# One multiply moved behind five DMA issues on ScalarE, in the expert loop of an AdaLN block

## The chip, the cores and the metric

The kernel runs on one core of a Trainium2 chip. The metric is device time in microseconds (us) from one launch, the median of several runs. Engines are named as in the profile: PE is TensorE, DVE is VectorE, ACT is ScalarE, POOL is GpSimd, SP is SyncE. "ACTq" rows are DMA issues by ScalarE's instruction queue.

## The reference, cut to what matters

The reference is one transformer block on x of shape (2, 4096, 512): layer norm and modulation, a linear-attention part, then a mixture of experts with 8 experts, of which each token takes two. The change touches the expert part alone:

```python
gate_out = ragged_dot(sorted_xs, w_gate, group_sizes=tokens_per_expert)   # 512 -> 2 x 512
activation = gelu(gate_out[:, 0, :]) * gate_out[:, 1, :]
expert_outputs = ragged_dot(activation, linear, group_sizes=tokens_per_expert)
out = einsum('blkd,blk->bld', expert_outputs per token, combine_weights)
x = x + gb * out            # gb: one row of 512 for each of the two batches
```

## The kernel before, in words

The program has three phases. The first makes keys and queries and splits the expert weights into a high and a low float32r part. The second finishes attention, routes the tokens and scatters token rows to one list per expert. The third, from about 1020 us to the end, is the expert loop; it walks 135 items (`ITEMS`), each one tile of 128 token rows of one expert. This text counts them 0 to 134, so the n-th row of any operation below that runs once per item belongs to item n-1.

For an item i the work is:

1. DVE turns the token rows (`turn_x`, L1597), ACT makes their high part (`x_hi`, L1015), DVE the low part (`x_lo`, L1603).
2. PE does the gate product and then the up product (`gate`, `up`: 12 matmuls each on L1721, three passes by four chunks).
3. ACT applies gelu to gate (`gelu`, L1020), DVE multiplies it with up (`glu`, L1609) into `hact`.
4. The activations have to be transposed. ACT stores `hact` to DRAM (`store_act`, one DMA, L1026, `act_rows<-hact`), later loads it back block by block in another order (`act_back`, four DMAs, L1033, `arow<-act_rows`), DVE transposes inside blocks (`turn_act`, L1615), ACT makes the high part (`act_hi`, L1039) and DVE the low part (`act_lo`, L1620).
5. PE does the down product (`down`, 12 matmuls, L1721 with `act_t_hi`).
6. DVE multiplies with the token's weight and its row of `gb` into `orow` (L1648), and POOL adds the rows to the output with an indirect DMA (L765). The row of `gb` is chosen by the token's batch: ACT makes `gb0`, the first batch's row times a 0/1 flag (`gb_rows`, L1045), and DVE adds the second batch's part (`gbr`, L1645).

The work is skewed over items by `LAG` = 3. In the loop's item i PE runs gate(i), up(i) and down(i-3). ACT runs `act_hi`(i-3), `gelu`(i), `x_hi`(i+1), `gb_rows`(i-3), `act_back`(i-1), `store_act`(i). DVE runs the small copies that end in `in_b` (`cur_of`, L1631 to L1635), `act_lo`(i-3), `turn_x`(i+1), `glu`(i), `x_lo`(i+1), `turn_act`(i-2), then `gbr` and `orow` of item i-3. Nothing but the order written in these functions sets the order on an engine; between engines there are semaphores.

The waits that matter here: `x_hi`(i+1) and `glu`(i) wait for up(i). `act_back`(i-1) waits until the store of item i-1 has landed in DRAM. `store_act`(i) waits for `glu`(i). `gb_rows` waits only for the flags of its item and for the `orow` of the item before. `gbr` waits for `gb_rows`, `orow` for down(i-3), and `act_lo` for `act_hi`. The down product waits for `act_lo`, the next gate product for `x_lo`. The weights of the next expert (three shares of about 3 MB and less) are loaded by SP's queue while items of the present one run.

Of the kernel before, what the change touches and what calls it, by code (L numbers as in the profile page):

```python
# [79 lines left out]
def at_least(eng, sem, value):  # L80

    if isinstance(value, int) and value <= 0:
        return
    eng.wait_ge(sem, value)
# [28 lines left out]
def build(nc, x, c_t, wmod, wqkv, wproj, b_proj, r_w, r_scale, pes, moe_w, out):  # L113
# [204 lines left out]
    def wait_apart(eng, sem, value):  # L318


        at_least(eng, sem, value)
        if not isinstance(value, int):
            eng.sem_inc(s_passed, 1)
# [450 lines left out]
    def _(act):  # L774
# [237 lines left out]
        def x_hi(i, at):  # L1012
            act.wait_ge(s_xt, i + 1)
            at_least(act, s_u, i)
            act.activation(x_t[0][:, :], XT_B[at % 2][:, :], ACT.Copy).then_inc(s_xthi, 1)  # L1015

        def gelu(i):
            act.wait_ge(s_g, i + 1)
            at_least(act, s_h, i)
            act.activation(gact[:, :], G_B[:, :], ACT.Gelu_apprx_tanh).then_inc(s_ga, 1)  # L1020

        def store_act(i, at):
            wait_apart(act, s_ar, 16 * NBLK * (i - RING + 1))
            wait_apart(act, s_h, i + 1)
            at = at % RING
            act.dma_start(ad[at * P:(at + 1) * P, :], hact[at % 2][:, :]).then_inc(s_hst, 16)  # L1026

        def act_back(i, at):
            wait_apart(act, s_ht, i - 1)
            wait_apart(act, s_hst, 16 * (i + 1))  # L1030
            at = at % RING
            for b in range(NBLK):
                act.dma_start(arow[at % 2][b * BLK:(b + 1) * BLK, :].rearrange("i (a n) -> i a n", a=NBLK),  # L1033
                              ad[at * P:(at + 1) * P, b * P:(b + 1) * P].rearrange("(a i) n -> i a n", a=NBLK)).then_inc(s_ar, 16)

        def act_hi(i):
            act.wait_ge(s_ht, i + 1)
            at_least(act, s_o, i)
            act.activation(act_t[0][:, :], HT_B[:, :], ACT.Copy).then_inc(s_hthi, 1)  # L1039

        def gb_rows(i, at):

            act.wait_ge(s_cur, 2 * (i + 1))
            at_least(act, s_or, i)
            act.activation(gb0[:, :], modbc[:, 0, 3, :], ACT.Copy, scale=in_b0[at % RING][:, 0:1]).then_inc(s_gb0, 1)  # L1045
# [6 lines left out]
        def item(i, at):  # L1052
            more = not isinstance(i, int) or i < ITEMS - 1
            lagging = not isinstance(i, int) or i >= LAG
            if lagging:
                act_hi(i - LAG)
            gelu(i)
            if more:
                x_hi(i + 1, at + 1)
            if lagging:  # L1060
                gb_rows(i - LAG, at - LAG)
            act_back(i - 1, at - 1)
            store_act(i, at)

        run_items(act, item)
        for i in range(ITEMS - LAG, ITEMS):
            act_hi(i)
# [985 lines left out]
```

## Time and profile before

| what | value |
|---|---|
| median of 3 runs | 2204.23 us (2200.72 to 2205.28) |
| the profiled execution's own time | 2204.23 us |
| span in its trace, first to last instruction | 2202.0 us |
| PE busy | 2082.6 us, 95% of the span |
| DVE, ACT, POOL busy | 60%, 36%, 36% |
| DMA queue q1 (SP), q10 (ACT), q0 (POOL) | 259.73, 70.82, 72.12 MB |

The profile is one execution. The span lies 2.2 us below the device time of the same execution. Busy time of PE is modelled and matmuls overlap. DMA issues are not counted as busy time of ACT; they stand in the timeline as ACTq rows, whose start is where the issue went out, not where data moved. In the timeline an entry may merge several instructions ("x3"); its second number is the time that it covers. A bracket at a row's end tells how long the engine was idle before it and what ended the idle time.

### The profile page before, as it was taken

How to read it: one execution, taken by the hardware profiler on the slowest of the kernel's cores; microseconds unless marked ns; L12 is line 12 of the kernel's file. 1: busy time of each engine (PE TensorE's matmuls, PEld its weight loads, DVE VectorE, ACT ScalarE, POOL GpSimd, SP SyncE). 2: the span in 40 equal slices, each digit the busy share in tenths (PEclk: the TensorE clock that was granted, in tenths of full speed). 3: DMA queues.
4: the chain of work that ended last, by engine and by line, in shares of the span. 5: the costliest groups of instructions: out<-in, count | busy, mean ns of one | idle time of the engine just before them, and what ended most of it. 6: DMA issues, size and time to landing. Idle time of an engine off the chain costs nothing.

```text
span 2202.0 us, 42565 instructions
## 1 busy us (share of the span) xinstructions
PE 2082.6 (95%) x9408; PEld 1618.8 (74%) x9409; DVE 1319.2 (60%) x3182; ACT 794.9 (36%) x1493; POOL 801.5 (36%) x618
## 2 busy tenths in 40 slices
PE   7999999999988999983999999999999989999997
PEld 4588887888855666662788888888878778888885
DVE  6555555556358787874555656565565555656554
ACT  3244443444335666651222222222222222222222
POOL 4466655665514667653111111111111111111111
PEclk9999999999989999996999999999999999999999
DMA  7575564556444767676855558558775975865554
GB/s 243 192 244 185 203 204 154 184 203 205 164 153 168 273 218 271 238 265 217 239 129 125 132 123 244 126 127 237 193 181 124 281 175 123 229 140 126 128 109 81
DMA packets 293689, 404.89 MB, mean 184 GB/s; under 512 B 50510, under 2 KB 188750, under 8 KB 285774
## 3 DMA queue, kind: packets, MB, share of 16 engines
q1 hardware_dynamic: 166256, 259.73, 37.0%
q0 software_dynamic: 30000, 72.12, 16.2%
q10 hardware_dynamic: 97200, 70.82, 10.1%
q14 instruction: 196, 1.61, 0.2%
q8 instruction: 37, 0.61, 0.1%
HBM read 210.57 MB, written 191.98 MB: 183 GB/s over the span
## 4 chain that ended last, share of the span: by engine, by line
PE 47%; DMA 3%; issue 1%; SPq 1%; ACTq 1%; DVE 0%; ACT 0%; POOL 0%; DVEq 0%; POOLq 0%
PE bank L1721 47%; DMA act_rows<-hact 2%; ACTq L1033 1%; DMA wbuf<-expert_split 0%; SPq L557 0%; DMA expert_rows<-rows,dest 0%; DMA out_rows<-orow,cur_tok 0%; DVE x_t_lo L1603 0%; DVE act_t_lo L1620 0%; ACT x_t_hi L1015 0%; DVE orow L1648 0%; SPq L555 0%; POOL expert_rows L744 0%; DMA arow<-act_rows 0%; DMA meta<-expert_rows 0%
## 5 line engine op out<-in xcount | busy, mean ns | idle before, releaser
L1721 PE MATMUL bank<-wbuf,x_t_hi 128*128 x2160 | 682.7, 397 | 33.5 <-DVE x_t_lo L1603 30.6
L765 POOL DMA_INDIRECT out_rows<-orow,cur_tok x135 | 209.0, 1548 | 971.8 <-DVE orow L1648 766.3
L1721 PEld LDWEIGHTS bank<-wbuf,x_t_hi 128*128 128x128 f32 x2160 | 409.0, 190 | 132.3 <-issue 35.4
L1721 PE MATMUL bank<-wbuf,x_t_lo 128*128 x1080 | 428.5, 397 | 0.0
L1721 PE MATMUL bank<-wbuf,act_t_hi 128*128 x1080 | 341.6, 397 | 13.4 <-DVE act_t_lo L1620 13.4
L1609 DVE TENSOR_TENSOR hact<-bank,gact 128x512 f32<-128x512 f32 x135 | 93.3, 691 | 379.6 <-PE bank L1721 369.9
L1721 PEld LDWEIGHTS bank<-wbuf,act_t_hi 128*128 128x128 f32 x1080 | 204.0, 189 | 64.8 <-issue 16.8
L1721 PEld LDWEIGHTS bank<-wbuf,x_t_lo 128*128 128x128 f32 x1080 | 204.7, 190 | 48.6
L1721 PE MATMUL bank<-wbuf,act_t_lo 128*128 x540 | 214.5, 397 | 0.0
L1015 ACT ACTIVATE x_t_hi<-bank 128x512 fp32r<-128x512 f32 x135 | 80.8, 599 | 299.2 <-PE bank L1721 285.3
L1039 ACT ACTIVATE act_t_hi<-bank 128x512 fp32r<-128x512 f32 x135 | 80.8, 598 | 289.7 <-DMA arow<-act_rows 202.6
L744 POOL DMA_INDIRECT expert_rows<-rows,dest x128 | 138.1, 1079 | 103.5 <-DVE dest L1424 69.1
L1020 ACT ACTIVATE gact<-bank 128x512 f32<-128x512 f32 x135 | 80.6, 597 | 252.6 <-PE bank L1721 232.3
L1122 DVE TENSOR_SCALAR hf<-bank,modcol 128x128 f32<-128x128 f32 x256 | 87.3, 402 | 94.5 <-PE bank L1701 94.4
L652 POOL TENSOR_TENSOR k_lo<-k_f,k_hi 128x512 fp32r<-128x512 f32 x64 | 89.0, 1390 | 122.3 <-ACT k_hi L817 122.2
L1721 PEld LDWEIGHTS bank<-wbuf,act_t_lo 128*128 128x128 f32 x540 | 102.3, 189 | 24.2
L648 POOL TENSOR_TENSOR z_lo<-xg,z_hi 128x512 fp32r<-128x512 f32 x64 | 83.3, 1304 | 98.2 <-ACT z_hi L806 98.2
L1648 DVE SCALAR_TENSOR_TENSOR orow<-bank,cur_w,gbr 128x512 f32<-128x512 f32 x135 | 101.4, 751 | 27.1 <-PE bank L1721 20.2
L1757 PE MATMUL bank<-k_hi,z_hi 128*128 128x512 f32 x256 | 104.4, 408 | 5.2 <-DVE kv L1206 2.9
L644 POOL TENSOR_TENSOR split_lo<-raw,split_hi 128x1536 fp32r<-128x1536 f32 x30 | 106.4, 3548 | 2.6 <-ACT split_hi L782 0.6
L1721 PE MATMUL bank<-kvp_hi,on_hi 128*128 128x512 f32 x256 | 103.5, 404 | 2.2 <-DVE on_lo L1525 2.2
L1597 DVE STREAM_TRANSPOSE bank<-xrow 128x512 f32<-128x512 f32 x135 | 96.8, 717 | 13.4 <-DMA meta<-expert_rows 13.4
(218 smaller groups left out, 3835.6 us busy)
## 6 DMA issues: line engine op xcount, KB each, us to landing
wbuf<-expert_split SPq DMA_DIRECT2D x24, 1536.0 KB
xrow<-expert_rows SPq DMA_DIRECT2D x540, 64.0 KB
act_rows<-hact ACTq DMA_DIRECT2D x135, 256.0 KB
arow<-act_rows ACTq DMA_DIRECT2D x540, 64.0 KB
expert_split<-split_hi SPq DMA_DIRECT2D x32, 768.0 KB, 3.6
expert_split<-split_lo SPq DMA_DIRECT2D x32, 768.0 KB, 5.9
xg<-in_x SPq DMA_DIRECT2D x16, 1024.0 KB, 5.4
q_rows<-qf SPq DMA_DIRECT2D x16, 1024.0 KB, 6.7
```

Of the source, the lines that this page charges most:

```text
L644: pool.tensor_tensor(sp_hl[1][:, :], raw[:, s, :], f32(sp_hl[0][:, :]), ALU.subtract).then_inc(s_elo, 1)
L648: pool.tensor_tensor(z_hl[1][:, t, :], xg[:, t, :], f32(z_hl[0][:, t, :]), ALU.subtract).then_inc(s_zlo, 1)
L652: pool.tensor_tensor(k_hl[t % 2][1][:, :], k_f[t % 2][:, :], f32(k_hl[t % 2][0][:, :]), ALU.subtract).then_inc(s_klo, 1)
L744: pool.indirect_dma_start(out=xs, out_offset=bass.IndirectOffsetOnAxis(dest[par][:, k, t:t + 1], 0), in_=rows[par][:, t, :], in_offset=Non ...
L765: pool.indirect_dma_start(out=out, out_offset=bass.IndirectOffsetOnAxis(cur_tok[at][:, 0:1], 0), in_=orow[at % 2][:, :], in_offset=None, c ...
L1015: act.activation(x_t[0][:, :], XT_B[at % 2][:, :], ACT.Copy).then_inc(s_xthi, 1)
L1122: last = ts(hf[t % 2][:, f, :], T_B[t % 2][:, f * P:(f + 1) * P], modcol[:, FC * B + at:FC * B + at + 1], modcol[:, at:at + 1], ALU.mult, ...
L1597: dve.transpose(XT_B[at % 2][:, :].rearrange("c (f a i) -> c a f i", f=FC, a=NBLK), xrow[at][:, :].rearrange("i (a f c) -> i a f c", a=NBL ...
L1609: tt(hact[at % 2][:, :], U_B[:, :], gact[:, :], ALU.mult).then_inc(s_h, 1)
L1648: stt(orow[at % 2][:, :], O_B[:, :], cur_w[at % RING][:, 0:1], gbr[:, :], ALU.mult, ALU.mult).then_inc(s_or, 1)
L1721: last = mm(dst, stationary(a, f), moving(b, f), start=(first and k == 0), stop=(k == parts * n - 1))
L1757: last = mm(ZK_B[f][:, :], z_hl[a][:, t, f * P:(f + 1) * P], k_hl[t % 2][b][:, :], start=(t == 0 and (a, b) == PASSES[0]), stop=(t == TPG ...
```

## The change

In the loop's item on ScalarE, `gb_rows`(i-3) is moved from ahead of `act_back`(i-1) and `store_act`(i) to behind them. The drain after the loop (`act_hi`, `act_back`, `gb_rows` for the last three items) is as before. All lines keep their numbers except these three in `item`.

```diff
             gelu(i)
             if more:
                 x_hi(i + 1, at + 1)
+            act_back(i - 1, at - 1)
+            store_act(i, at)
             if lagging:
                 gb_rows(i - LAG, at - LAG)
-            act_back(i - 1, at - 1)
-            store_act(i, at)
```

ScalarE, one item of the unrolled start of the expert loop (every later item reads alike). `act_stored` is the landing of the store, `act_ready` is `glu`, `down_done` the down product:

```order
 L1020 ACTIVATE gact<-bank2 128x512 [waits act_ready,gate_done]
 L1015 ACTIVATE x_t_hi<-bank5 128x512 [waits up_done,x_turned]
-L1045 ACTIVATE gb0<-modbc,in_b0_1 128x512 [waits out_rows_ready,cur_ready]
 L1033 DMA arow1<-act_rows 32x4x128 [waits act_stored,act_turned]
 L1033 DMA arow1<-act_rows 32x4x128 x3
 L1026 DMA act_rows<-hact0 128x512 [waits act_ready,act_rows_loaded]
+L1045 ACTIVATE gb0<-modbc,in_b0_1 128x512 [waits out_rows_ready,cur_ready]
 L1039 ACTIVATE act_t_hi<-bank1 128x512 [waits down_done,act_turned]
```

The multiply now stands behind a DMA that waits for a landing, and directly ahead of `act_hi`. The orders of PE, DVE, POOL and SP are unchanged.

VectorE, the engine that consumes `gb0`, before and now the same, in the last items of the loop. `gb0_ready` is the moved multiply, `gb_rows_step` the row after it:

```order
L1603 TENSOR_TENSOR x_t_lo<-bank0,x_t_hi 128x512 [waits up_done,x_hi_ready]
L1615 STREAM_TRANSPOSE bank1<-arow1 128x4x4x32 [waits act_lo_ready,act_rows_loaded]
L1645 SCALAR_TENSOR_TENSOR gbr<-modbc,in_b1_2,gb0 128x512 [waits cur_ready,gb0_ready,rows_added,out_rows_ready]
L1648 SCALAR_TENSOR_TENSOR orow0<-bank4,cur_w2,gbr 128x512 [waits gb_rows_step,down_done]
L1627 TENSOR_LOAD tables
L1627 ISA x2
L1631 ISA [waits rows5_loaded,rows_added,out_rows_ready]
L1631 COPY cur_w1<-meta5 128x1
L1632 COPY cur_tok5<-meta5 128x1
L1634 TENSOR_SCALAR in_b0_1<-cur_tok5 128x1 [waits cur_step]
L1635 TENSOR_SCALAR in_b1_1<-cur_tok5 128x1
L1620 TENSOR_TENSOR act_t_lo<-bank1,act_t_hi 128x512 [waits act_hi_ready]
```

Nothing moved here; the rows show what stands in line between `gbr` and the next `act_lo`, for which PE's down product waits.

## Rows read from the trace of the kernel before

**Rows 1.** The chain of waits over the whole span, its shares by line

```profile
by line: PE bank L1721 47.1%; DMA act_rows<-hact 2.4%; issue 1.0%; ACTq L1033 0.6%; DMA wbuf<-expert_split 0.4%; SPq L557 0.3%; DMA expert_rows<-rows,dest 0.3%; DMA out_rows<-orow,cur_tok 0.2%; DVE x_t_lo L1603 0.1%; DVE act_t_lo L1620 0.1%
```

**Rows 2.** Waits of PE, 1030 to 2202 us: total, times, longest

```profile
PE bank L1721 <- DVE act_t_lo L1620: 13.4, 7, 3.3
```

**Rows 3.** The chain of waits, 1500 to 1800 us: start, us, what

```profile
1600.65 9.06 DMA act_rows<-hact
...
1747.15 12.73 DMA act_rows<-hact
```

**Rows 4.** Timeline of a quiet item (46): start, us, engine, line, operation, idle before

```profile
1421.27 0.60 ACT L1015 ACTIVATE x_t_hi<-bank 128x512 fp32r<-128x512 f32 x1 [2.18 <-PE bank L1721]
1421.67 0.31 ACTq L1033 DMA_DIRECT2D arow<-act_rows  x1
1421.77 0.72 ACT L1045 ACTIVATE gb<-modbc,in_b 128x512 f32<-128x512 f32 x1
...
1423.69 0.34 ACTq L1026 DMA_DIRECT2D act_rows<-hact  x1
...
1421.30 0.69 DVE L1609 TENSOR_TENSOR hact<-bank,gact 128x512 f32<-128x512 f32 x1 [3.01 <-PE bank L1721]
...
1423.14 0.71 DVE L1645 SCALAR_TENSOR_TENSOR gbr<-modbc,in_b,gb 128x512 f32<-128x512 f32 x1
1423.99 0.75 DVE L1648 SCALAR_TENSOR_TENSOR orow<-bank,cur_w,gbr 128x512 f32<-128x512 f32 x1
...
1425.32 0.68 DVE L1620 TENSOR_TENSOR act_t_lo<-bank,act_t_hi 128x512 fp32r<-128x512 f32 x1
...
1429.66 0.69 DVE L1609 TENSOR_TENSOR hact<-bank,gact 128x512 f32<-128x512 f32 x1 [3.02 <-PE bank L1721]
...
1429.37 0.62 PE L1721 MATMUL bank<-wbuf,act_t_hi 128*128 x2
```

**Rows 5.** Timeline of ACT in item 1, where no gb_rows stands between

```profile
1044.60 0.60 ACT L1015 ACTIVATE x_t_hi<-bank 128x512 fp32r<-128x512 f32 x1 [2.25 <-PE bank L1721]
1044.63 1.78 ACTq L1033 DMA_DIRECT2D arow<-act_rows  x4
```

**Rows 6.** The chain of waits behind a late store, item 87

```profile
1784.58 0.34 ACTq L1026
...
1785.04 0.61 ACT act_t_hi L1039
...
1785.66 0.70 DVE act_t_lo L1620
...
1786.82 3.29 PE bank L1721 x13
```

**Rows 7.** Timeline of the last item: DVE waits for gb_rows there

```profile
2189.00 0.72 ACT L1045 ACTIVATE gb<-modbc,in_b 128x512 f32<-128x512 f32 x1 [0.19 <-DVE orow L1648]
...
2189.86 0.75 DVE L1645 SCALAR_TENSOR_TENSOR gbr<-modbc,in_b,gb 128x512 f32<-128x512 f32 x1 [0.32 <-ACT gb L1045]
```

**Rows 8.** Timeline: stores of items 3, 38, 57, and each next glu

```profile
1065.80 0.44 ACTq L1026 DMA_DIRECT2D act_rows<-hact  x1
...
1069.85 0.69 DVE L1609 TENSOR_TENSOR hact<-bank,gact 128x512 f32<-128x512 f32 x1 [1.55 <-PE bank L1721]
...
1359.44 0.34 ACTq L1026 DMA_DIRECT2D act_rows<-hact  x1
...
1362.74 0.69 DVE L1609 TENSOR_TENSOR hact<-bank,gact 128x512 f32<-128x512 f32 x1 [0.83 <-DMA act_rows<-hact]
...
1518.64 0.34 ACTq L1026 DMA_DIRECT2D act_rows<-hact  x1
...
1521.68 0.69 DVE L1609 TENSOR_TENSOR hact<-bank,gact 128x512 f32<-128x512 f32 x1 [0.23 <-PE bank L1721]
```

**Rows 9.** DMA queues, 1502 to 1503 us, weights loading: packets, MB, share of engines

```profile
q1 hardware_dynamic: 31, 0.38, 90.3%
q10 hardware_dynamic: 25, 0.05, 13.1%
```

## The prediction, made before the changed kernel ran

> **What bounds the kernel now.** I read the chain of waits first. By line it is mostly PE's products, and the largest piece that is not PE is a DMA, the store of the activations, 2.4% of the span [rows 1]. So the expert loop is bound by PE, and the only other thing that now and then takes over is the store's landing. Second, the waits of PE in the expert loop: it waits for `act_lo` 7 times, 13.4 us in all, the longest 3.3 [rows 2]; all other items run at PE's pace. Third, the chain between 1500 and 1800 us, which shows where: stores whose way to the next `act_back` took 9.06 and 12.73 us [rows 3]. Fourth, the timeline of a quiet item, to see how much room the other engines have [rows 4]: `glu` starts at 1421.30, the next at 1429.66, so the period is 8.36 us. The down product that needs this item's `act_lo` begins at 1429.37, which is 8.07 after `glu` and 0.29 before the next one. I call this moment D and measure lateness of everything against it.
>
> **The change in a quiet item.** ScalarE has the same 135 multiplies of 0.72 us and the same DMAs; nothing is added. Two things shift.
>
> First, the DMA issues come earlier. With `gb_rows` between, the first `act_back` goes out 0.40 us after `x_hi` began (1421.27 to 1421.67) [rows 4]; where no `gb_rows` stood between, 0.03 us after [rows 5]. The gain is at most 0.37 us and at least nothing. The loop body has a register operation there which the early item lacks, so I take 0.30. Note that it is not 0.72: the issue at 1421.67 goes out before the multiply begins at 1421.77, so the multiply's run itself never delayed the DMAs, only its dispatch. The store, now at 1423.69, will go at about 1423.39.
>
> Second, `gb_rows` comes later. It now follows the store's issue as `act_hi` did, 0.46 us after it (1784.58 to 1785.04) [rows 6], so at 1423.85 in place of 1421.77. `gbr` can follow 0.86 us after the multiply's start, read at the one place where DVE really waited for it [rows 7]: 1424.71 in place of 1423.14. `orow` follows `gbr` by 0.85 (1423.14 to 1423.99), `act_lo` follows `orow` by 1.33, with the four small copies between them [rows 4]. So `act_lo` starts at 1424.71 + 0.85 + 1.33 = 1426.89, 1.57 later than now. PE can start 1.16 after `act_lo`'s start (1785.66 to 1786.82) [rows 6], so at 1428.05, and D is at 1429.37. 1.32 us are left. A quiet item therefore costs nothing: the delay hides under the up product. It also gains nothing, since PE was never waiting there. The rows added to the output go out 1.6 us later; only POOL's next scatter waits for them, and `orow` two items on, for its buffer.
>
> **The change in a late item.** Here the path has no cover. `act_back`(i-1) sits on ScalarE's queue until the store of item i-1 has landed, and now `gb_rows` sits behind it. Before, the multiply, `gbr` and `orow` were all done in the shadow of that wait, and after the store's issue only `act_hi` and `act_lo` remained: from the store's issue to PE 1786.82 - 1784.58 = 2.24 us [rows 6]. Now DVE has `gbr`, `orow` and the small copies still in front of `act_lo`: 0.46 + 0.86 + 0.85 + 1.33 + 1.16 = 4.66 us. That is 2.42 more, against at most one early start of 0.30 for a run of late items: net 2.12. The chain from store to landing to `act_back` to next store does not itself pass through `gb_rows`, so within a run of late items the loss is not repeated; it is paid once, at the last.
>
> So an item costs something as soon as its store is issued later than D - 4.66, in place of D - 2.24. Item by item, D being the next `glu` less 0.29:
>
> Item 3, the first with a `gb_rows`: its store goes at 1065.80, set by a store of item 2 that nothing moved, so no early start is subtracted. 1065.80 + 4.66 = 1070.46 against D = 1069.56: 0.90 us [rows 8].
> Item 38: 1359.44 - 0.30 + 4.66 = 1363.80 against 1362.45: 1.35 us [rows 8].
> Item 57: 1518.64 - 0.30 + 4.66 = 1523.00 against 1521.39: 1.61 us [rows 8].
> The run of late stores that holds the 9.06 us landing, and the run that begins with the 12.73 us one and ends at item 87, both make PE wait already [rows 3, 6]: 2.12 each, 4.24.
>
> Sum: 0.90 + 1.35 + 1.61 + 4.24 = 8.1 us. The drain is not touched, except that the last loop item's `orow` may come a tenth later. Made against the profiled execution, 2204.23 us, which is also the median of the runs, this gives 2212.3 us.
>
> Bounds of the terms: with the early start at 0 or 0.37 in place of 0.30, the four last runs of lateness cost 1.2 more or 0.3 less. With `gbr` following the multiply by 0.72, its bare duration, in place of 0.86, all five cost 0.7 less. Each landing differs from run to run: the three times before lie 4.6 us apart, and the late items are the only place in the loop where I see such room.
>
> **A rule that bears on it.** While weights load, the two queues' packets move nearly one for one: 31 packets of q1 with 0.38 MB and 25 of q10 with 0.05 MB in one microsecond [rows 9]. So a store that meets a weight load waits for one large packet before each small one of its own. The Trainium skill states the same as a rule, in "DMA: Bandwidth & Descriptors", section "Queues, rings and completion order": each DMA engine goes round the queues that have work and switches at packet boundaries. By that rule a store that is issued 0.30 us earlier gets at most about one packet's turn ahead and still shares the engines for the rest; the 8.1 us would stand. Without it, if the earlier store simply went ahead of the weights, the second rival below would be the result.
>
> **The rivals.**
>
> *The late items thin out, no change.* The stores of items 38 and 57 are late by chance of where a weight share meets them. If their landings come 1.4 and 1.7 us sooner, both terms vanish, and if the three landings of the last run are 0.7 shorter each its 2.12 goes as well: 8.1 - 1.35 - 1.61 - 2.12 = 3.0, so 2207.2 us. For it: lateness in most of the loop is zero, and few items decide. Against it: nothing in the change makes landings shorter by more than the 0.30.
>
> *Faster: the store overtakes.* One mechanism: stores 0.30 earlier, and the scatter of output rows 1.6 us later, leave `act_rows` free of other traffic, and the landings of 9.06 and 12.73 us [rows 3] fall to what fits under the period. It decides from the point where the landings of a run shrink together by more than the 2.12 that the run costs. If it were complete, PE's waits for `act_lo` would go but for those of the drain. I put three of the 7 there, for its three last down products, at the mean of all: 13.4 x 4/7 = 7.7 goes [rows 2], and 2204.2 - 7.7 = 2196.5 us. Against it stand the packets that alternate [rows 9].
>
> *Slower by more: the scatter moves into the way.* Rows added 1.6 us later compete with the loading of the activations just stored, which was free of them. If some six stores in the crowded stretches land 1 us later each, that adds up to 6 us: 2218 us. For it: in such a stretch every microsecond of landing goes straight to PE. Against it: in quiet items there is room for it.
>
> **How the numbers follow.** The forecast, 2209 to 2216 us, gets 0.45. Thinned-out late items 0.28, overtaking 0.12, the scatter in the way 0.15. What can be told from no change here is about 0.2%, 4.4 us either way. The first and the last of these cases are slower by more than that, 0.60; the second is no change, 0.28; overtaking is faster, 0.12. The range that leaves out 2 in 10 is 2202 to 2218 us. Predicted is the likeliest, 2212.3 us.
>
> **What would show it.** In a quiet item of the changed kernel: first `act_back` issue about 0.1 us after `x_hi` begins; `gb_rows` about 2.5 us after `glu`, after the store; `orow` no longer started by PE's down product but by `gbr`, 1.5 us later than now; PE without a gap. In a late item: the chain of waits runs store issue, `gb`, `gbr`, `orow`, `act_lo`, PE, about 4.7 us in place of 2.2, and PE's waits for `act_lo` rise from 7 to about 10, their sum by about 8 us. The prediction is wrong if `gb_rows` never appears on the chain, if the landings of the stores change by more than 1 us on average, or if `gbr` follows quickly enough that `act_lo` still waits for `act_hi` last.

## The result, and the profile after

| | before | after |
|---|---|---|
| median of 4 runs | 2202.47 us (2196.64 to 2205.28) | 2227.73 us (2217.87 to 2236.43) |
| the profiled execution, its span | 2204.23 us, 2202.0 us | 2228.31 us, 2226.2 us |
| ratio after / before | | 1.0104, interval 1.0073 to 1.0137 |

The changed kernel is slower, as forecast, but by 25 us and not by 8; the time lies outside the range of the prediction. A second timing of the same kernel gave 1.0068 [1.0042, 1.0094], which is 15 us, so what has to be explained is 15 to 25 us.

**A quiet item.** The timeline of item 46 after the change, ACT first, then DVE (columns as in [rows 4], which show the same item before):

```profile
1434.12 0.60 ACT L1015 ACTIVATE x_t_hi<-bank 128x512 fp32r<-128x512 f32 x1 [2.19 <-PE bank L1721]
1434.36 1.83 ACTq L1033 DMA_DIRECT2D arow<-act_rows  x4
1436.44 0.34 ACTq L1026 DMA_DIRECT2D act_rows<-hact  x1
1436.96 0.72 ACT L1045 ACTIVATE gb<-modbc,in_b 128x512 f32<-128x512 f32 x1 [2.24 <-DMA arow<-act_rows]
1437.59 0.58 ACT L1039 ACTIVATE act_t_hi<-bank 128x512 fp32r<-128x512 f32 x1
...
1434.14 0.69 DVE L1609 TENSOR_TENSOR hact<-bank,gact 128x512 f32<-128x512 f32 x1 [1.15 <-PE bank L1721]
...
1437.81 0.75 DVE L1645 SCALAR_TENSOR_TENSOR gbr<-modbc,in_b,gb 128x512 f32<-128x512 f32 x1 [1.74 <-ACT gb L1045]
1438.67 0.75 DVE L1648 SCALAR_TENSOR_TENSOR orow<-bank,cur_w,gbr 128x512 f32<-128x512 f32 x1
...
1440.01 0.68 DVE L1620 TENSOR_TENSOR act_t_lo<-bank,act_t_hi 128x512 fp32r<-128x512 f32 x1
...
1442.54 0.69 DVE L1609 TENSOR_TENSOR hact<-bank,gact 128x512 f32<-128x512 f32 x1 [1.22 <-PE bank L1721]
```

The next `glu` comes 8.40 us after this one, so PE has its old pace. The first `act_back` goes out 0.24 after `x_hi` (0.40 before), the store 2.30 after `glu` (2.39 before), so the early start is 0.16 at the first DMA and 0.09 at the store (0.04 at the store in the median of all items). `gb` starts 0.52 after the store, `gbr` 0.85 after `gb`, `act_lo` 5.87 after `glu` where it was 4.02. The bracket behind `gbr` is new: DVE now waits for the multiply. Over the loop the waits of DVE (total us, times, longest) have this at their top, where before it came only once, in the last item, with 0.3 us:

```profile
DVE gbr L1645 <- ACT gb L1045: 225.5, 120, 5.1
```

**A late item.** The chain of waits after the change, item 68, behind three landings in a row, of 9.05, 8.98 and the 8.31 us in the first line; its own store was issued at 1631.35:

```profile
1620.83 8.31 DMA act_rows<-hact
...
1630.64 1.21 DMA arow<-act_rows
...
1631.87 0.73 ACT gb L1045
...
1632.72 0.76 DVE gbr L1645
...
1633.58 0.76 DVE orow L1648
...
1635.09 0.61 DVE act_t_lo L1620
...
1636.14 2.08 PE bank L1721 x7
```

From the store's issue to PE it is 1636.14 - 1631.35 = 4.79 us, against 2.24 in [rows 6]. In item 36 it is again 4.79. Over all items in which PE waits for `act_lo` it is 4.45 to 5.8 us in the two traces of after, and 2.2 to 2.6 in the two of before; the two waits behind store 57, in item 58, have 5.35 and 5.31.

**Where the time is.** The first and last rows of `glu` from item 3 to item 134 (131 periods), after and then before:

```profile
1067.99 0.69 DVE L1609 TENSOR_TENSOR hact<-bank,gact 128x512 f32<-128x512 f32 x1 [3.17 <-PE bank L1721]
...
2196.96 0.69 DVE L1609 TENSOR_TENSOR hact<-bank,gact 128x512 f32<-128x512 f32 x1 [1.87 <-PE bank L1721]
```

```profile
1061.48 0.69 DVE L1609 TENSOR_TENSOR hact<-bank,gact 128x512 f32<-128x512 f32 x1 [4.77 <-PE bank L1721]
...
2173.50 0.69 DVE L1609 TENSOR_TENSOR hact<-bank,gact 128x512 f32<-128x512 f32 x1 [3.69 <-PE bank L1721]
```

Against 131 quiet periods of 8.365 us (1095.8) the loop takes 33.2 us more after the change and 16.2 before. The second traces of each give 29.7 and 13.5. So the loop costs 16.6 us more in the mean of two traces each. In the profiled pair another 6.5 us lie ahead of item 3; there the traces of before differ by 5.2 among themselves (item 3 at 1061.48 and 1066.71), and the second trace of after has it at 1059.76, ahead of both, so I count none of that to the change.

Where a period was longer than the quiet one by over 0.5 us, in us, from the starts of `glu`:

| items | before, two traces | after, two traces | more, mean | my term |
|---|---|---|---|---|
| 4 | 0, 0 | 2.1, 0 | 1.0 | 0.90 (store of 3) |
| 37, 38 | 0, 0 | 3.7, 3.7 | 3.7 | 1.35 (store of 38) |
| 58 | 0, 0 | 2.1, 2.1 | 2.1 | 1.61 (store of 57) |
| 67 to 70 | 0.6, 4.6 | 8.7, 5.9 | 4.7 | 2.12 |
| 84 | 4.6, 3.9 | 7.4, 7.1 | 3.0 | none |
| 86 to 88 | 8.7, 4.6 | 3.9, 8.2 | -0.6 | 2.12 (run ending at 87) |
| 104, 106 | 0, 0 | 3.1, 1.1 | 2.1 | none |
| sum | | | 16.0 | 8.1 |

In item 84 PE waits for the next expert's weights in both kernels; the matmul that waits there is the gate product's first, which does not read `act_lo`. PE's waits in the loop, 1080 to 2180 us, after and then before:

```profile
PE bank L1721 <- DVE act_t_lo L1620: 15.7, 8, 2.5
PE bank L1721 <- DMA wbuf<-expert_split: 5.2, 1, 5.2
```

```profile
PE bank L1721 <- DVE act_t_lo L1620: 9.7, 5, 3.3
PE bank L1721 <- DMA wbuf<-expert_split: 2.8, 1, 2.8
```

That is 6.0 us more for `act_lo`, 2.4 more for weights; in the second traces it is 9.9 more for `act_lo` (15.5 and 5.6) and 2.7 more for weights (4.8 and 2.1). A wait of 2.1 us in item 4 of this trace of after lies ahead of the window. It is put down to the weights, but `act_lo` had started 1.13 us before PE went on, as in every wait for `act_lo`. A large part of the rest is clock. Item 38 after the change lost its time without waiting for anything: two stretches of it, and the same part of the loop before (columns: length, then busy us and instructions of PE, PEld, DVE, ACT, POOL, then the granted clock of PE, DMA share, GB/s):

```profile
1358.00:1360.00 2.00, 2.00 (x6) 1.61 (x5) 0.79 (x2) 0.17 (x1) 0.00 (x0) 0.50 1.03 381
1360.00:1362.00 2.00, 2.00 (x8) 1.54 (x8) 1.21 (x2) 1.15 (x2) 0.00 (x0) 0.70 0.94 257
```

```profile
1357.00:1361.00 4.00, 4.00 (x19) 3.25 (x18) 2.14 (x7) 1.05 (x2) 0.21 (x1) 1.00 0.84 144
```

At a granted clock of 0.50 (1.2 GHz of 2.4) PE completes 6 matmuls in 2 us, where before it had 19 in 4. PE had stood still for `act_lo` until 1356.62, for 1.88 us, and the clock fell after that. Where such a fall takes in an item without a wait of its own, the item is 1.8 to 1.9 us longer (item 38 in both traces of after, item 70 in one trace of each kernel, item 87 in one of after). Item 106 is not one of them: PE waited 1.95 us there at full clock. From item 4 to item 134 PE has 17.1 us at the half clock in each trace of after, and 6.8 and 10.2 in the two of before, so 3 to 5 us more are lost to it. In the profiled pair 6.0 + 2.4 + 2.1 + 5 = 15.5 of 17.0; the rest is in no row that I found.

**What the prediction did not have: the weights.** SP loads token rows and weights, and one item's weight share stands behind token rows that wait for the small copies (`in_b`, L1635). Those copies stand behind `orow` on DVE. Waits of SP in the loop, after and before:

```profile
SPq L323 <- DVE in_b L1635: 143.6, 82, 3.4
```

```profile
SPq L323 <- DVE in_b L1635: 120.7, 67, 5.7
```

The weight load in item 34, then the store of item 35 and the `act_back` that waits for its landing, after and before (`glu` of item 34 at 1329.77 and 1320.91):

```profile
1334.69 1.03 SPq L530 DMA_DIRECT2D wbuf<-expert_split  x2
...
1340.58 0.34 ACTq L1026 DMA_DIRECT2D act_rows<-hact  x1
...
1349.76 0.31 ACTq L1033 DMA_DIRECT2D arow<-act_rows  x1
```

```profile
1324.17 1.03 SPq L530 DMA_DIRECT2D wbuf<-expert_split  x2
...
1331.83 0.34 ACTq L1026 DMA_DIRECT2D act_rows<-hact  x1
...
1339.28 1.79 ACTq L1033 DMA_DIRECT2D arow<-act_rows  x4
```

The load starts 4.92 us after `glu` where it was 3.26, and the store lands in 9.18 us where it took 7.45. (A landing is read here from the store's issue to the first `act_back` behind it. In a quiet item that is 6.2 to 6.4 us whatever the store does, since `act_back` isn't due sooner.) The same holds behind other items at which a load starts: landings went from 7.5 to 9.1 (item 65) and from under 7 to 8.5 (item 102). That the queues share the engines is in [rows 9], 31 packets of q1 to 25 of q10. With the rule of the Trainium skill ("DMA: Bandwidth & Descriptors", section "Queues, rings and completion order") that an engine goes round its queues packet by packet, the longer landing fits with more of the load lying beside the store; no trace here shows how much did. I had used that rule only for the store's own 0.30 us, not for a load that moves 1.66; how long a landing gets, the rule does not give.

### The profile page after: what moved, and what is told of

Read it like the earlier page. It is cut to its first block, busy times and chain, and to the rows that moved or that the text cites. A ratio compares the mean times of both kernels' runs of the same rounds, so it can differ in the third digit from the quotient of the medians.

```text
span 2226.2 us, 42565 instructions
## 1 busy us (share of the span) xinstructions
PE 2096.0 (94%) x9408; PEld 1630.7 (73%) x9409; DVE 1343.1 (60%) x3182; ACT 794.8 (36%) x1493; POOL 802.0 (36%) x618
## 3 DMA queue, kind: packets, MB, share of 16 engines
q14 instruction: 196, 1.61, 0.2%
## 4 chain that ended last, share of the span: by engine, by line
PE 43%; DMA 5%; SPq 2%; issue 1%; ACTq 1%; DVE 1%; POOL 0%; ACT 0%; DVEq 0%; POOLq 0%
PE bank L1721 43%; DMA act_rows<-hact 3%; DMA out_rows<-orow,cur_tok 1%; ACTq L1033 1%; SPq L557 1%; DMA wbuf<-expert_split 1%; DVE gbr L1645 0%; DVE orow L1648 0%; ACT gb L1045 0%; DVE act_t_lo L1620 0%; SPq L555 0%; POOL expert_rows L744 0%; DMA arow<-act_rows 0%; SPq L559 0%; DMA expert_rows<-rows,dest 0%
## 5 line engine op out<-in xcount | busy, mean ns | idle before, releaser
L1645 DVE SCALAR_TENSOR_TENSOR gbr<-modbc,in_b,gb 128x512 f32<-128x512 f32 x135 | 101.5, 752 | 254.3 <-ACT gb L1045 232.8
L1045 ACT ACTIVATE gb<-modbc,in_b 128x512 f32<-128x512 f32 x135 | 97.7, 724 | 338.3 <-DMA arow<-act_rows 170.7
```

Source lines behind the costliest of these rows:

```text
L1645: gbs.did(stt(gbr[:, :], modbc[:, 1, 3, :], in_b1[at % RING][:, 0:1], gb0[:, :], ALU.mult, ALU.add))
```

## The experiments

The table has each kernel's median, its ratio to the kernel before on the same chip with the interval, the start of item 34's weight load after `glu`, and the landing of item 35's store (where another item is named, of that item's store).

| kernel | us | ratio | weights start | landing |
|---|---|---|---|---|
| after_again | 2217.67 | 1.0068 [1.0042, 1.0094] | 4.85 | 8.87 |
| before_again | 2203.86 | 1.0001 [0.9982, 1.0020] | 3.25 | 7.86 |
| pre_late | 2205.03 | 1.0018 [0.9993, 1.0042] | 3.22 | 7.4 |
| pre_early | 2202.87 | 1.0000 [0.9982, 1.0018] | 3.25 | 7.2 |
| orow4 | 2216.54 | 1.0084 [1.0056, 1.0112] | 4.94 | 9.0 |
| lo_first | 2224.59 | 1.0114 [1.0091, 1.0137] | 6.3 | 10.4 |
| orow4_lo | 2221.12 | 1.0098 [1.0067, 1.0129] | 6.3 | 10.2 |
| back_first_pre | 2221.83 | 1.0115 [1.0084, 1.0145] | 3.0 | 8.8 |
| cur_late | 2213.85 | 1.0037 [1.0015, 1.0059] | 4.1 | 8.1 |
| cur_later | 2207.99 | 1.0005 [0.9986, 1.0025] | 4.4 | 8.4 |
| cur_early_a | 2234.25 | 1.0141 [1.0113, 1.0169] | 2.4 | 6.9; item 55, load at 0.5: 14.9 |
| cur_early_b | 2220.12 | 1.0068 [1.0043, 1.0093] | 1.2 | item 34: 12.9 |
| cur_early_pre | 2223.56 | 1.0097 [1.0069, 1.0125] | 1.2 | item 34: 13.0 |
| cur_mid | 2231.26 | 1.0121 [1.0092, 1.0150] | 4.4 | 8.3 |
| shares4_b | 2234.60 | 1.0130 [1.0104, 1.0156] | | |
| shares4_a | 2241.87 | 1.0169 [1.0140, 1.0197] | | |
| wfirst_b | 2211.22 | 1.0024 [0.9995, 1.0054] | 4.2 | 7.8 |
| wfirst_a | 2219.22 | 1.0066 [1.0037, 1.0094] | 4.4 | 8.6 |

### The two kernels again

No edit but an empty line at the end of the file.

> The changed kernel once more, for a second trace. In its first trace the expert loop began 6.5 us later than in the trace of before, for a reason that lies ahead of the changed lines, and the loop itself took 17 us more. If the late start is chance, this trace starts its loop at another time and the median stays at 2218 to 2236 us; if the change causes it (code placed elsewhere), the loop starts near 1067 us at item 3's glu again.

> The kernel before once more, for a second trace: 2197 to 2206 us. If the number of late stores is chance, their items and landings differ from those of the first trace, while the sum of PE's waits in the loop stays under 20 us.

The loss is real and its size is 15 to 25 us; the kernel before against itself shows nothing. The late start of the loop was chance.

### Keep the early DMAs, take the multiply out of DVE's way

`gb0` gets two buffers, and the multiply is made one item ahead. In pre_late it stands where the change put it, behind the store; in pre_early ahead of the DMAs, where it was.

```diff
+            act_back(i - 1, at - 1)
+            store_act(i, at)
+            if ahead:
+                gb_rows(i - LAG + 1, at - LAG + 1)
-            if lagging:
-                gb_rows(i - LAG, at - LAG)
-            act_back(i - 1, at - 1)
-            store_act(i, at)
```

> gb_rows stands behind the DMAs as in the changed kernel, but works one item ahead (item i-2) into one of two buffers, so VectorE finds its result ready. Theory A (what costs is that gbr, orow, the scatter and act_lo wait for gb_rows): back to 2198 to 2207 us. Rival B (the DMAs sent 0.1 to 0.3 us earlier collide with other traffic): stays above 2218 us. Rival C (the multiply now ahead of act_hi on ScalarE delays act_hi by about 0.6 us in late items): 2206 to 2212 us.

> gb_rows one item ahead into one of two buffers, but ahead of the DMAs as in the kernel before. Theory A: VectorE did not wait for it before, so no change, 2197 to 2206 us. It is the control for the two buffers: if it moves, the look-ahead itself does something.

PE's waits in the loop of pre_late:

```profile
PE bank L1723 <- DVE act_t_lo L1622: 7.4, 3, 3.1
PE bank L1723 <- DMA wbuf<-expert_split: 2.4, 1, 2.4
```

The loss is gone within the interval, which leaves room for 0.42%, with the DMAs issued as early as in the change and the multiply at the same place in ScalarE's queue; in the trace the loop takes 9.9 us over its quiet pace, against 16.2 and 13.5 before. DVE's 225 us of waiting for `gb` are gone too, and the weight load is back at 3.22. So the cause is `gbr` waiting for the multiply, with everything that this wait delays. The earlier DMAs do neither good nor harm that this measurement shows, and pre_early against pre_late says the same.

### Is it the buffer of orow?

The chain of waits of after passes several times through the scatter of output rows, as here in item 36:

```profile
1347.60 5.61 DMA out_rows<-orow,cur_tok
1353.21 0.75 DVE gbr L1645
```

That reads as if `gbr` waited for the scatter to free its buffer. orow4 gives the buffer four copies.

```diff
-            at_least(dve, s_add, 16 * (i - 1))
+            at_least(dve, s_add, 16 * (i - 3))
...
-            stt(orow[at % 2][:, :], O_B[:, :], cur_w[at % RING][:, 0:1], gbr[:, :], ALU.mult, ALU.mult).then_inc(s_or, 1)
+            stt(orow[at % 4][:, :], O_B[:, :], cur_w[at % RING][:, 0:1], gbr[:, :], ALU.mult, ALU.mult).then_inc(s_or, 1)
```

> The changed kernel with four buffers for orow in place of two. gbr and orow then wait for a scatter two items older, so the 20 us in which gbr waited for out_rows in both traces of the changed kernel should be gone, while gbr still waits for gb_rows. Theory A1 (both waits feed PE's stalls: the late gb_rows and, on top, the scatter's landing): part of the loss returns, 2207 to 2213 us, with PE's waits for act_lo reduced but longer than before. Rival A2 (the order gb_rows, gbr, orow, act_lo is all that matters): no change from the changed kernel, 2216 to 2220 us. Rival A3 (the scatter's landing is all): 2202 us.

Waits of DVE in orow4:

```profile
DVE gbr L1646 <- ACT gb L1046: 223.5, 120, 6.8
...
DVE gbr L1646 <- DMA out_rows<-orow,cur_tok: 24.6, 9, 3.9
```

It is as slow as the change, and the wait is still put down to the scatter, 24.6 us, although now a scatter two items further back would have to be late. It was a false releaser: in every one of these items `gb` started 0.83 to 0.86 us before `gbr`, which is the delay of the quiet items (0.85). `gbr` waits for the multiply always.

### Take act_lo's way out instead

lo_first makes `act_lo` ahead of `gbr` and `orow` on DVE, and gives the down product a second bank. orow4_lo is both edits.

```diff
-            if lagging:
-                act_lo(i - LAG)
...
                 turn_act(i - LAG + 1, (at - LAG + 1) % DEPTH)
+                act_lo(i - LAG + 1)
             if lagging:
                 out_rows(i - LAG, (at - LAG) % DEPTH)
```

> The changed kernel, but VectorE makes act_lo(i-2) before gbr and orow of item i-3, and the down product has two banks so that it needn't wait for orow. gb_rows is as late as in the changed kernel, gbr still waits for it and for the scatter. Theory A (the loss reaches PE through act_lo queued behind gbr and orow): back to 2198 to 2206 us, although gbr goes on waiting. Rival (the late scatter harms by its traffic, in landings of the stores): stays above 2210 us.

> Both at once: four orow buffers, and act_lo ahead of gbr. Theory A: as lo_first within 3 us, since a wait of gbr no longer reaches PE in either. If the scatter's wait also delayed glu and x_lo of the next item, this is 3 us or more faster than lo_first.

PE's waits in lo_first:

```profile
PE bank L1720 <- DVE x_t_lo L1603: 8.7, 7, 1.9
PE bank L1720 <- DMA wbuf<-expert_split: 7.8, 1, 7.8
PE bank L1720 <- DVE act_t_lo L1620: 4.2, 4, 1.5
```

The waits for `act_lo` are down from 15.7 to 4.2, and the kernel is as slow as the change. `orow` and the small copies now come later still, so the weight load starts at 6.3 and the store lands in 10.4; and DVE gets to the next tokens late (`x_lo`). The edit moved the loss and did not remove it, and my expectation for it was wrong. With four buffers on top (orow4_lo) it is the same within the intervals. It is no clean test of `act_lo`'s way, but it was the first sign that the small copies matter by themselves.

### The store ahead of the next tokens

```diff
             gelu(i)
+            act_back(i - 1, at - 1)
             if more:
                 x_hi(i + 1, at + 1)
-            act_back(i - 1, at - 1)
```

> gb_rows one item ahead into two buffers, behind the store, and act_back(i-1) moved ahead of x_hi(i+1), so that the store of item i no longer stands behind four DMA issues (1.9 us). A store is then issued about 1.6 us earlier after glu and late stores have that much more room. If the late stores' chain is what is left of PE's waits, 2192 to 2199 us; rival: act_back now holds up x_hi when a landing is late, so PE waits for x_lo in place of act_lo and nothing is gained, 2200 to 2206 us.

```profile
PE bank L1723 <- DVE x_t_lo L1605: 13.6, 7, 2.9
PE bank L1723 <- DMA wbuf<-expert_split: 1.8, 1, 1.8
```

Slower by 1.15%, where no loss had been expected. The DMA that waits for a landing now holds back `x_hi`, and PE waits for `x_lo` 7 times where it had waited for `act_lo`. It is the same lesson in another place: what stands behind the waiting DMA inherits every late landing.

### The small copies and the weight loads alone

cur_late moves the copies of the kernel before behind `act_lo` and `turn_x`, so that the weights start later with `act_lo` as early as ever. cur_later adds a spare multiply ahead of them.

```diff
-            cur_of(i - 1, (at - 1) % DEPTH)
             if lagging:
                 act_lo(i - LAG)
             if more:
                 turn_x(i + 1, (at + 1) % DEPTH)
+            ts(spare[0][:, :], modbc[:, 0, 3, :], 1.0, None, ALU.mult)   # cur_later alone
+            cur_of(i - 1, (at - 1) % DEPTH)
```

> The kernel before, with only the small copies of cur_of (L1631 to L1635) moved on VectorE behind act_lo and turn_x, about 1.3 us later. gb_rows, gbr, orow and act_lo are as early as before or earlier. Theory P (SP's queue waits for these copies before it loads the rows of a later item, and the weight loads stand behind that; a weight load that starts later meets the store of the activations): the weight load of item 34 starts 1.3 us later than in the kernel before (3.3 us after glu there), the store of item 35 lands about 1.3 us later, and the time rises by 3 to 10 us. Rival Q (the loss comes only from act_lo waiting behind gb_rows, gbr and orow): no change or faster, 2197 to 2203 us.

> As cur_late (the kernel before with the copies of cur_of behind act_lo and turn_x), with a spare 128x512 multiply ahead of the copies that writes to a buffer of its own: a second dose. gb_rows, gbr, orow and act_lo are as early as before. The weight load of item 34 starts about 4.9 us after glu, as in the changed kernel. Theory P: the loss is larger than cur_late's 0.37%, 8 to 16 us over before, with landings of 9 us in items 35, 56, 65, 102 as in the changed kernel. Rival: no more than cur_late.

PE's waits in cur_later:

```profile
PE bank L1723 <- DMA wbuf<-expert_split: 6.0, 1, 6.0
PE bank L1723 <- DVE act_t_lo L1621: 3.3, 1, 3.3
```

Landings grow (8.1 and 8.4, against 8.9 and 9.2 in the change), item 84 is longer (8.3 and 8.6 us against 3.9 to 4.6), and no period at items 37, 58 or 104 is long; the loop costs 13.5 and 13.8 us over its quiet pace, as before. By the timings late weights alone cost between nothing (cur_later) and 0.4% (cur_late), and the 8 to 16 us expected for cur_later didn't come. The one with the smaller delay came out slower, and neither load starts as late as the 4.9 us of the change, so I take no more from the pair than "a few us at most, for half to 0.7 of the delay".

The opposite: the copies of item i ahead of `gbr`, in after (a), before (b) and pre_late (pre).

```diff
-            cur_of(i - 1, (at - 1) % DEPTH)
...
                 turn_act(i - LAG + 1, (at - LAG + 1) % DEPTH)
+            cur_of(i, at)
             if lagging:
                 out_rows(i - LAG, (at - LAG) % DEPTH)
```

> The changed kernel, with the copies of cur_of(i) moved ahead of gbr, so that SP no longer waits for orow while act_lo still stands behind gb_rows, gbr and orow. Theory P and the lateness of act_lo together: the weight load of item 34 starts no later than 3.3 us after glu, the store of item 35 lands as early as in the kernel before, and the time falls from 2218 to 2203 to 2211 us; what is left is act_lo's part, worth up to 8 us. Rival Q: stays at 2215 us or more, less 0.4 us per late item for the shorter way from orow to act_lo.

> The kernel before, with the copies of cur_of(i) ahead of gbr. Theory P: SP's weight loads start about 1.7 us earlier than in the kernel before, PE's wait for the weights (3.9 to 4.6 us in four traces) becomes 1.7 us shorter and late stores are fewer: 2192 to 2200 us. Rival Q: no change, 2198 to 2204 us.

> gb_rows one item ahead into two buffers and behind the store (pre_late), and the copies of cur_of(i) ahead of gbr. Theory P: like cur_early_b, 2192 to 2200 us, since neither VectorE's wait nor SP's is left. If gb_rows ahead of act_hi on ScalarE costs something in late items, up to 3 us slower than cur_early_b.

PE's waits in cur_early_b:

```profile
PE bank L1721 <- DVE act_t_lo L1620: 13.5, 4, 4.2
PE bank L1721 <- DMA wbuf<-expert_split: 1.8, 1, 1.8
```

All three got slower than the kernel they came from, by 0.4 to 0.8% by the ratios, where each had been expected to be faster. In cur_early_b and cur_early_pre the weights start 1.2 us after `glu`, ahead of this item's own store, which then takes 12.9 us (issued 1336.28, `act_back` at 1349.16 in cur_early_b); PE stalls behind the stores of items 34, 55, 64 and 101, 3 to 4 us each in cur_early_b. In cur_early_a the load of item 34 came at 2.4 and the stores of items 34 and 35 landed within 6.4 and 6.9; behind the other three, where it came at 0.5, PE stalls 5.6 to 6.9 us each. The wait for the weights themselves is 1.8 us in cur_early_b and 4.7 in cur_early_a. So the landing goes with the start of a weight load relative to the store: 12 to 15 us at 0.5 to 1.2, 6.9 to 7.7 at 2.4, 7.5 at 3.3, 9 at 4.9, 10.4 at 6.3. The kernel before, with most of its loads at 2.4 to 3.3, sits in the good place. As a test of the change these kernels fail, since they add a stall of their own.

cur_mid tried to put the copies at the old distance by letting them wait for the multiply:

```diff
             if lagging:
+                dve.wait_ge(s_gb0, i - LAG + 1)
+            cur_of(i, at)
+            if lagging:
                 out_rows(i - LAG, (at - LAG) % DEPTH)
```

> The changed kernel, with cur_of(i) ahead of gbr but made to wait for gb_rows first, so that it ends about 4.1 us after glu, as in the kernel before. gb_rows, gbr, orow and act_lo are as late as in the changed kernel. If the start of the weight loads relative to the stores carries the loss, the weight load of item 34 starts 3.0 to 3.6 us after glu, the store of item 35 lands within 8 us, and the time is 2 to 8 us above before (2 to 8 being what act_lo's way alone costs by the prediction's sum). Rival Q (act_lo's way carries it all): 14 us or more above before.

Inconclusive: the extra wait pushed `act_lo` to 6.8 us after `glu` in the median item, which takes all but 0.1 us of its room (PE's down product starts at 8.07 and needs it 1.16 sooner), and the load moved only from 4.9 to 4.4.

### Smaller weight shares

```diff
-SHARES = (GATE_UP[0:2], GATE_UP[2:3], DOWNS)
+SHARES = (GATE_UP[0:1], GATE_UP[1:2], GATE_UP[2:3], DOWNS)
```

> The kernel before, with the next expert's weights asked for in four shares, one an item, in place of three (the first of 3 MB is cut in two of 1.5 MB). If 3 MB bursts against stores are what makes landings late, late stores become fewer: 2 to 8 us faster than before. Rival: the last share comes an item later and PE waits longer for the weights of the short expert: same or slower.

> The changed kernel with the same four shares. If a burst met at a bad moment is the cause, smaller bursts take away most of the difference between the two orders: within 8 us of shares4_b. Rival Q: the difference of 15 us remains.

PE's waits in shares4_b, then in shares4_a:

```profile
PE bank L1721 <- DMA wbuf<-expert_split: 39.7, 2, 26.3
```

```profile
PE bank L1721 <- DMA wbuf<-expert_split: 22.5, 2, 15.2
PE bank L1721 <- DVE act_t_lo L1620: 17.0, 5, 5.5
```

Four shares take one item more to load, and a short expert's successor is not there in time: 39.7 us of waiting. No wait for `act_lo` is left in b, 17.0 us in a. The expected gain didn't come. The change costs 0.39% on top of b here, though the two intervals overlap.

### The same weight timing for both

In both kernels SP issues the weights ahead of the token rows and waits for the same event, a moment that lies ahead of `orow`'s copies.

```diff
         def step(i, at):
-            load_rows(i, at)
+            wait_apart(sp, s_h, i - AHEAD + 1)
             next_weights(i - AHEAD)
+            load_rows(i, at)
```

> The kernel before, but SP's step waits for glu of the item in hand and asks for weights first, and only then loads the rows of the item seven ahead. The weight loads are then paced by glu and no longer by the copies of cur_of; the load of item 34 starts about 3 us after glu. Close to the kernel before, 2196 to 2210 us: it is the base for wfirst_a.

> The changed order on ScalarE with the same step on SP: weight loads start as in wfirst_b within 0.3 us, while act_lo still stands behind gb_rows, gbr and orow. The difference to wfirst_b is what act_lo's way costs by itself. If it is all of the loss: 14 us or more over wfirst_b. If the late weight loads are a part: 5 to 11 us over wfirst_b. If it costs nothing without them: within 4 us.

PE's waits in wfirst_b, then in wfirst_a:

```profile
PE bank L1722 <- DMA wbuf<-expert_split: 8.5, 1, 8.5
PE bank L1722 <- DVE act_t_lo L1621: 6.0, 2, 3.0
```

```profile
PE bank L1722 <- DVE act_t_lo L1621: 6.6, 6, 2.1
PE bank L1722 <- DMA wbuf<-expert_split: 5.4, 2, 4.1
```

With the weights at 4.2 and 4.4 us, the change costs 8.0 us by the medians and 0.42% (9 us) by the ratios; the two intervals overlap, so this is a size and not a proof. The traces don't confirm it as a sum: the loop takes 21.1 us over its quiet pace in wfirst_a and 18.9 in wfirst_b, only 2.2 of the 7.6 us by which the two spans differ. Nor are the loads at one timing everywhere: wfirst_b asks for one share only in item 83 (wfirst_a in 82), and its item 84 costs 10.3 us where that of wfirst_a costs 6.7. The places are plainer than the sum: wfirst_a has long periods at items 37 (1.3), 58 (1.5) and 104 (0.6), wfirst_b has none there. (The trace puts the 1.3 us of item 37 down to the weights; `act_lo` had started 1.13 us before PE went on, so it is a wait for `act_lo`.) One item shows why. Behind the landing of item 35, the store of item 36 is issued so long after its `glu`: 3.70 us in before (4.09 in its second trace), 4.08 in wfirst_b, 4.75 in cur_later, 4.78 in wfirst_a, 5.33 in after. With the short way it may go until 8.07 - 2.24 = 5.83, with the long way until 8.07 - 4.79 = 3.28. So cur_later loses nothing (4.75 under 5.83), wfirst_a at nearly the same moment should lose 1.5 (measured 1.3), after 2.0 (1.8), and after with its store as early as in before would lose 0.4 (0.8 by the second trace). At this item the long way makes the loss possible, and by this reckoning the later weights make most of its size.

The output rows go out later in wfirst_a than in wfirst_b, and its landings over 7 us are not longer in sum: together they exceed 7 by 15.6 us, in wfirst_b by 21.8. That of item 35 alone is longer, 8.6 for 7.8.

## Why the prediction was wrong in size

**Right: the mechanism and who pays.** The change costs PE time only where a landing is late, through `gb`, `gbr`, `orow`, the small copies and `act_lo`. Removing `gbr`'s wait alone removes the loss (pre_late). The way measured 4.79 us at its plainest against 4.66 forecast; quiet items cost nothing, as forecast; item 58 lost 2.1 us for 1.61. PE's waits for `act_lo` rose by 6.0 and 9.9 us in the two pairs of traces, for the 8 forecast.

**Luck.** Item 4 lost 2.1 us in one trace and nothing in the other, so its mean of 1.0 for 0.90 says little. The term of 2.12 for the run ending at item 87 was not met: items 86 to 88 lost 0.6 us less than before. Item 84, for which the sum has no term, lost 3.0 more in the wait for weights and the slow clock behind it, and the two nearly cancel. In the trace before, PE already waited 2.8 us for these weights, and the prediction, which names the waits for `act_lo` alone, does not mention it. The 8 to 9 us of the timings with weights asked for first lie near the 8.1, but their traces put only 2.2 of it into the loop, so they don't confirm the sum.

**Wrong, the step that failed: "Item by item".** I took the set of late stores, and how late they are, from the trace before, and let the change only lengthen the way behind them. That needs every landing to stay as it was. The step rests on a sentence on the quiet item: the output rows go out 1.6 us later, and "only POOL's next scatter waits for them, and `orow` two items on, for its buffer". That leaves out the copies that stand directly behind it on DVE and SP's queue that waits for them. The weight load of item 34 moved by 1.66 us, the landing behind it grew by 1.0 to 1.7, and item 36 became late where it had not been; the item 38 of my sum is not the one that lost. Items 37 and 38, 67 to 70, and 104 and 106 cost 3.7, 4.7 and 2.1 instead of 1.35, 2.12 and nothing: 7.0 us more than the sum, nearly all of the 7.9 between 16.0 and 8.1. That each of these lost time through a longer landing is shown in the rows for item 37 alone; for the other two it fits with the landings that grew behind the loads of items 64 and 101.

**Left out: the clock after a stall.** Each stall of some 2 us was priced at its own length. Behind some of them an item lost another 1.8 to 1.9 us at a granted clock of 0.50, 3 to 5 us more over the loop than before. The trace before had 6.8 us of such time, and I did not look for it.

**Too large: the early start.** 0.09 us at the store for the 0.30 taken, so the lower bound of nothing was the nearer one. By my own bounds that adds 0.8 us to four terms.

**The rivals.** The thin-out is false: the landings of the items behind a weight load grew, although the mean over all items rose by only 0.05 us (6.40 to 6.45), far under the 1 us that the prediction named as a sign of being wrong. "The store overtakes" is false for the same reason, and pre_late, which has the early DMAs with everything else as before, gains nothing. "The scatter moves into the way" had the right sign and place, longer landings in crowded stretches, but the wrong traffic: late weights alone lengthen the landing (cur_late, cur_later), and with nearly equal weights the later scatter makes them no longer in sum (wfirst_a). The latter is one trace each; the scatter was not moved by itself.

**What stays open.** How the 15 to 25 us divide. The pair with nearly equal weights gives 8 to 9 us to the way by its timings and 2.2 by its traces; late weights alone, by up to 1.2 of the 1.66 us, cost 0 to 0.4%; what remains is their meeting, longer landings that count only because the room for the store's issue fell from 5.83 to 3.28 us. That they meet is shown at item 37; how much it comes to over the loop was not measured by itself. No kernel tried is faster than the kernel before beyond its interval; pre_early equals it.

## What to carry to other kernels

Before moving an instruction behind a DMA issue that waits for a landing, follow its consumer's engine down to everything queued behind that consumer, however small, and ask which other queue waits for it: here four copies of 0.15 us gated 3 MB of weights. If a cheap operand is wanted early by another engine, make it one item ahead into a second buffer; then its place in the queue made no difference here (pre_late, pre_early). A sum over late items taken from one trace holds only while the landings stay as they are, which a change in the start of large transfers ends; here the sum came out at half of what was measured. A new stall of PE can cost more than its length, since the slow clock may follow it.

## What the runs showed of the hardware

A DMA issue is not held up by an ACTIVATE that is still running: with nothing between, `act_back` went out 0.24 us after `x_hi` began, and `x_hi` ran 0.60. With an ACTIVATE queued between it was 0.40, so that in item 46 its dispatch cost 0.16 and its 0.72 us of work nothing.

The landing of a 256 KB store went with the start of a 3 MB load relative to it, and not monotonically: 13 us, 7.5, 9 and 10.4 for loads that start 1.2, 3.3, 4.9 and 6.3 us after `glu`. The store is this item's at 1.2 and the next one's at the others.

Behind some waits of about 2 us the granted clock of TensorE fell to 0.50 of full, 1.2 to 1.6 us after the engine had gone on working; the matmuls of the stretch show it, 6 in 2 us. In the trace of after it fell behind waits of 1.88, 1.76 and 2.07 us (items 37, 69, 86) and not behind those of 2.10, 2.16, 2.07, 2.52 and 1.95 (items 4, 58, 67, 68, 106). In the wait of 5.18 us (item 84) it fell while the engine stood still.

The releaser that the profile names for a wait on several semaphores can be wrong for many microseconds together: 24.6 us in orow4 were put down to a scatter that freed a buffer nobody was short of, and the waits of item 4 in after and of item 37 in wfirst_a to weights, where `act_lo` ended them.
